# Giving a product a second pair of inputs instead of adding a trace, with four small edits around the router

## The reference

```
ctx    = ema(x, tau_ctx);  wg = sigmoid([x, ctx] @ Wg + bg);  gated = x * wg
mod    = 0.5 + sigmoid(gelu(x @ Wn1 + bn1) @ Wn2 + bn2)            # 8 values for each token
traces = ema(gated * mod[..., d], tau[d])  for d in 0..7
temporal = sum over d of traces[d] * softmax(blend)[d]
gate   = sigmoid(temporal @ Wtemp + btemp);  soma = gelu(x @ Wsoma + bsoma)
out    = (soma * gate) @ Wout;  z = layernorm(out) * gamma + beta
logits = z @ router.T;  top 8 of 64 experts, their softmax weights scaled to sum 1
expert e takes its first 128 tokens: silu(z @ Wgate) * (z @ Wup) @ Wdown, times the weight, added to each token
shared expert on all z;  x + routed + shared is the output
```

## Time and profile before

| what | us |
|---|---|
| median of three runs | 1110.4 |
| lowest and highest | 1106.49, 1114.75 |
| the profiled execution | 1111.76 |
| its span | 1110.0 |
| the conditioning pipeline in the trace | about 500 to 845 |
| the routed experts | about 852 to 1086 |

### The profile page before, as it was taken

The page is one execution under the profiler, slowest core; times in us unless marked ns, Lnnn a source line. Parts: engine busy times, 40 slices in busy tenths (PEclk is TensorE's granted clock), DMA queues, the critical chain, the costliest instruction groups (busy, mean ns, idle before and its releaser), DMA issues.

```text
span 1110.0 us, 14852 instructions
## 1 busy us (share of the span) xinstructions
PE 952.2 (86%) x4544; PEld 663.8 (60%) x4544; DVE 746.3 (67%) x1522; ACT 460.8 (42%) x835; POOL 667.0 (60%) x498
## 2 busy tenths in 40 slices
PE   5969899999999999987369889888688999889960
PEld 2534699899998999863125454444453665556640
DVE  2658466666666676524778999999876777667620
ACT  0320444555445544443446675757322222223320
POOL 1113444555445554315999999999852577777870
PEclk9989999999999999998689999999878999999995
DMA  4879234444344442134213742343259699996557
GB/s 153 276 261 349 63 77 113 90 89 95 87 118 86 89 100 39 21 66 105 96 38 96 245 150 69 114 138 117 90 167 320 179 262 264 259 254 144 94 72 156
DMA packets 93142, 155.46 MB, mean 140 GB/s; under 512 B 15784, under 2 KB 73328, under 8 KB 89936
## 3 DMA queue, kind: packets, MB, share of 16 engines
q1 hardware_dynamic: 51280, 90.61, 25.0%
q0 software_dynamic: 25296, 40.52, 20.3%
q10 hardware_dynamic: 16496, 23.49, 6.3%
HBM read 119.56 MB, written 43.42 MB: 147 GB/s over the span
## 4 chain that ended last, share of the span: by engine, by line
POOL 12%; issue 11%; PE 9%; DMA 7%; DVE 6%; ACT 2%; DVEq 2%; POOLq 2%; ACTq 0%
DMA odd_rows<-ys,slots 5%; POOL wide L652 4%; POOL wide L660 3%; DVE wide L1295 3%; PE bank L1685 3%; POOL xg L745 2%; DMA out<-ys,slots 2%; POOL out L752 1%; PE bank L1923 1%; DMA xg<-z_rows,slots 1%; POOL odd_rows L752 1%; POOLq L640 1%; ACT zrow L969 1%; ACT wide L919 1%; PE bank L1752 1%
## 5 line engine op out<-in xcount | busy, mean ns | idle before, releaser
L652 POOL TENSOR_TENSOR wide<-wide 128x1024 f32<-128x1024 f32 x64 | 156.6, 2461 | 31.8 <-issue 31.8
L1295 DVE TENSOR_TENSOR_SCAN wide<-bank,wide 128x512 f32<-128x512 f32 x128 | 149.4, 1210 | 22.3 <-POOL wide L652 22.1
L895 ACT ACTIVATE h_raw<-bank,b 128x512 f32<-128x512 f32 x128 | 88.1, 689 | 168.7 <-PE bank L1658 166.3
L1232 DVE TENSOR_TENSOR h_lo<-h_raw,h_hi 128x512 fp32r<-128x512 f32 x128 | 87.3, 692 | 91.8 <-ACT h_hi L899 91.8
L1673 PE MATMUL bank<-w_hi,h_hi 128*128 128x256 f32 x512 | 144.4, 282 | 0.1
L1673 PE MATMUL bank<-w_lo,h_hi 128*128 128x256 f32 x512 | 142.2, 278 | 0.0
L1673 PE MATMUL bank<-w_hi,h_lo 128*128 128x256 f32 x512 | 142.1, 278 | 0.0
L623 POOL DMA_INDIRECT x_rows<-ob,put x64 | 110.3, 1723 | 28.3 <-issue 16.0
L660 POOL TENSOR_TENSOR wide<-wide 128x1024 f32<-128x1024 f32 x46 | 108.4, 2358 | 11.9 <-issue 8.1
L919 ACT ACTIVATE wide<-wide,blend 128x512 f32<-128x512 f32 x128 | 84.0, 715 | 62.1 <-POOL wide L652 58.5
L1658 PE MATMUL bank<-ex_hi,w_hi 128*128 128x512 f32 x256 | 99.7, 389 | 2.5 <-issue 2.5
(11 more groups left out here) (242 smaller groups left out, 2002.6 us busy)
## 6 DMA issues: line engine op xcount, KB each, us to landing
wide<-in_mwp SPq DMA_DIRECT2D x40, 512.0 KB, 4.3
wide<-m_rows SPq DMA_DIRECT2D x16, 1024.0 KB, 4.8
w1s<-in_fW SPq DMA_DIRECT2D x8, 1024.0 KB, 5.0
w2s<-in_fW SPq DMA_DIRECT2D x8, 1024.0 KB, 5.3
own<-in_mwp SPq DMA_DIRECT2D x15, 512.0 KB, 4.9
head<-in_mwp SPq DMA_DIRECT2D x9, 512.0 KB, 4.3
xT<-in_xT ACTq DMA_DIRECT2D x8, 512.0 KB, 4.5
xt<-in_x ACTq DMA_DIRECT2D x8, 512.0 KB, 6.8
```

Source lines behind the costliest of these rows:

```text
L652: G.tensor_tensor(drive[n % DRIVES], gb[d % 2], md[d // HD][:, d % HD, :].unsqueeze(1).to_broadcast([P, CT, S]), ALU.mult).then_inc(c_u, 1)
L895: A.activation(h1_raw[f % 4][:, :], bank[:, 2 + f % 4, :], ACT.Gelu_apprx_tanh, bias=b1_0[:, bass.ds(e, 1), f]).then_inc(b_h, 1)
L1232: V.tensor_tensor(h1_lo[:, f, :], h1_raw[f % 4][:, :], h1_hi[:, f, :].bitcast(F32), ALU.subtract).then_inc(b_lo, 1)
L1295: o = V.tensor_tensor_scan(dst[:, c, :], decay[:, d:d + 1].to_broadcast([P, S]), drive[(D * b + d) % DRIVES][:, c, :], 0.0, ALU.mult, ALU.add)
```

## The change

Five edits come together.

1. Trace 7 is no longer added. `temp_in` takes `acc` and the ring buffer of trace 7 as four inputs of one accumulated product, the second pair with the same weights. Eight matmuls stand where four stood. Six adds stay for each sequence, one of them on VectorE. The buffer of trace 7 is given back by the product (`c_tem`) and not by an add. Two other waits, of SyncE's weight loads and of GpSimd's memsets in the last step, go from the last add to the last product.
2. Two small operations of `rstd_of` go from GpSimd to ScalarE (`moments`), ahead of `wg_out`.
3. The 0/1 mask of chosen experts is made on ScalarE with Sign and Relu (`chosen_out`) instead of a comparison and a copy on VectorE. For the last sequence VectorE writes it with one comparison.
4. The expert weights are stored without the division by their sum. The reciprocal of the sum goes into one more column, and each expert multiplies by it when it picks up its weight.
5. Rows of `z_rows` have 324 floats instead of 320.

```diff
-ZW = H + E1
+ZW = H + E1 + 4
...
 def added(b, d):
+    return level((D - 2) * b + d - 1)
...
     if b == B:
         weight_store(B - 2)
-        sp.wait_ge(c_add, added(B - 1, D - 1))
+        sp.wait_ge(c_tem, level(B - 1))
...
 def rstd_of(q):
-    pool.wait_ge(c_mv, level(q))
+    pool.wait_ge(c_mw, level(q))
     pool.wait_ge(c_no, level(q - 1, TT))
-    G.tensor_scalar(veps1[:, :], mv1[:, :, 1], 4 * EPS, None, ALU.add)
-    G.tensor_scalar(shift1[:, :], mv1[:, :, 0], -1.0, None, ALU.mult)
-    pool.drain()
...
     if on(b - 1) and b != B:
         add_trace(b - 1, 6)
-    if on(b - 1) and b != B:
-        add_trace(b - 1, 7)
...
+def moments(q):
+    act.wait_ge(c_mv, level(q))
+    act.wait_ge(c_no, level(q - 1, TT))
+    A.activation(veps1[:, :], mv1[:, :, 1], ACT.Copy, bias=4 * EPS)
+    A.activation(shift1[:, :], mv1[:, :, 0], ACT.Copy, scale=-1.0).then_inc(c_mw, 1)
...
+def chosen_out(q):
+    act.wait_ge(c_top, level(q))
+    A.activation(sign[:, :, :], rep[:, :, :], ACT.Sign, bias=far[:, :], scale=-1.0)
+    act.drain()
+    A.activation(chosen(q), sign[:, :, :], ACT.Relu).then_inc(c_ma, 1)
...
     if on(b):
         weighted(b, 7)
+    if on(b - 1):
+        moments(b - 1)
     if ahead(b + 1):
         wg_out(b + 1)
...
-    dve.drain()
-    V.tensor_tensor(mask[:, :, :], rep[:, :, :], lgp, ALU.not_equal).then_inc(c_top, 1)
-    dve.drain()
-    V.tensor_copy(mask_all[:, :, q * TT:(q + 1) * TT].rearrange("p e t -> p t e"), mask[:, :, :])
+    if q < B - 1:
+        o.then_inc(c_top, 1)
+    else:
+        dve.drain()
+        V.tensor_tensor(chosen(q), rep[:, :, :], lgp, ALU.not_equal).then_inc(c_top, 1)
...
-    V.tensor_tensor(mask[:, :, :], mask[:, :, :], ex[:, :, :], ALU.mult)
+    V.scalar_tensor_tensor(zrow[:, :, H:H + E1], rep[:, :, :], -1.0e38, ex[:, :, :], ALU.is_lt, ALU.mult)
...
-    V.reciprocal(wsum[:, :], wsum[:, :])
-    dve.drain()
-    V.tensor_tensor(zrow[:, :, H:ZW], mask[:, :, :], wsum[:, :].unsqueeze(2).to_broadcast([P, TT, E1]),
-                    ALU.mult).then_inc(c_zr, 1)
+    V.reciprocal(zrow[:, :, H + E1], wsum[:, :]).then_inc(c_zr, 1)
...
-    V.tensor_copy(share[i][:, :], xg1[e % ROWS][:, H + e:H + e + 1])
+    V.tensor_tensor(share[i][:, :], xg1[e % ROWS][:, H + e:H + e + 1], xg1[e % ROWS][:, H + E1:H + E1 + 1], ALU.mult)
...
 def temp_in(q):
-    pe.wait_ge(c_add, added(q, D - 1))
+    pe.wait_ge(c_add, added(q, D - 2))
+    pe.wait_ge(c_scan, level(D * q + D - 1))
     if q + 2 < B:
         pe.wait_ge(c_x1T, level(q + 2))
     pe.wait_ge(c_fin, level(q - 2))
-    project(4, wtemp, [acc[q % 2][:, 0, :], acc[q % 2][:, 1, :]]).then_inc(c_tem, 1)
+    last = trace[((D - 1) * q + D - 2) % TRACES]
+    project(4, wtemp, [acc[q % 2][:, 0, :], acc[q % 2][:, 1, :], last[:, 0, :], last[:, 1, :]]).then_inc(c_tem, 1)
```

More of the change, by code:

```diff
@@ L222, in build @@
         neg = sb("neg", [P, TT, E1])
-        mask = sb("mask", [P, TT, E1])
+        sign = sb("sign", [P, TT, E1])
+        far = sb("far", [P, 1])
         ex = sb("ex", [P, TT, E1])
@@ L282, in prep_start, with chosen @@
             return 4 * k - 8 - (0 if k < 4 else 1 if k == 4 else 2)
+        def chosen(q):
+            return mask_all[:, :, q * TT:(q + 1) * TT].rearrange("p e t -> p t e")
         def z_bank(q):
@@ L339, in build @@
         c_mdl = [sem(f"c_mdl{n}", 16) for n in range(2)]
+        c_mw = sem("c_mw")
+        c_ma = sem("c_ma")
         c_pad, e_pad = sem("c_pad", 0), sem("e_pad", 0)
@@ L710, in step @@
                 if b == B:
-                    pool.wait_ge(c_add, added(B - 1, D - 1))
+                    pool.wait_ge(c_tem, level(B - 1))
                     for r in range(FREED):
@@ L997, in step @@
                     exponentials(B - 2)
+                    chosen_out(B - 2)
                     shared_b_out(B - 2)
@@ L1000, in step @@
                     shared_out(B - 2)
+                    moments(B - 1)
                     normalise(B - 1)
@@ L1029, in step @@
                     exponentials(b - 2)
+                    chosen_out(b - 2)
                 if on(b):
@@ L1291, in scan_unit @@
                     n = (D - 1) * b + d - 1
-                    dve.wait_ge(c_add, level(n - TRACES))
+                    old, of = divmod(n - TRACES, D - 1)
+                    if of == D - 2:
+                        dve.wait_ge(c_tem, level(old))
+                    else:
+                        dve.wait_ge(c_add, added(old, of + 1))
                     dst = trace[n % TRACES]
@@ L1352, in pick @@
                     to_exponents()
+                dve.wait_ge(c_ma, level(min(q - 1, B - 2)))
                 for j in range(TT):
-                    V.match_replace(rep[:, j, :], top8[:, j, :], lgp[:, j, :], -3.0e38)
-                dve.drain()
-                V.tensor_tensor(mask[:, :, :], rep[:, :, :], lgp, ALU.not_equal).then_inc(c_top, 1)
-                dve.drain()
-                V.tensor_copy(mask_all[:, :, q * TT:(q + 1) * TT].rearrange("p e t -> p t e"), mask[:, :, :])
+                    o = V.match_replace(rep[:, j, :], top8[:, j, :], lgp[:, j, :], -3.0e38)
+                if q < B - 1:
+                    o.then_inc(c_top, 1)
+                else:
+                    dve.drain()
+                    V.tensor_tensor(chosen(q), rep[:, :, :], lgp, ALU.not_equal).then_inc(c_top, 1)
                 if q == B - 1:
@@ L1380, in route_weights @@
                 dve.wait_ge(c_zwt, level(q - 1, 16))
-                V.tensor_tensor(mask[:, :, :], mask[:, :, :], ex[:, :, :], ALU.mult)
+                V.scalar_tensor_tensor(zrow[:, :, H:H + E1], rep[:, :, :], -1.0e38, ex[:, :, :], ALU.is_lt, ALU.mult)
                 dve.drain()
-                V.tensor_reduce(wsum[:, :], mask[:, :, :], AX.X, ALU.add)
+                V.tensor_reduce(wsum[:, :], zrow[:, :, H:H + E1], AX.X, ALU.add)
                 dve.drain()
-                V.reciprocal(wsum[:, :], wsum[:, :])
-                dve.drain()
-                V.tensor_tensor(zrow[:, :, H:ZW], mask[:, :, :], wsum[:, :].unsqueeze(2).to_broadcast([P, TT, E1]),
-                                ALU.mult).then_inc(c_zr, 1)
+                V.reciprocal(zrow[:, :, H + E1], wsum[:, :]).then_inc(c_zr, 1)
             def finish(q):
@@ L1436, in drain_share @@
                 add_trace(B - 1, 6)
-                add_trace(B - 1, 7)
                 pick(B - 2)
@@ L1505, in front_only @@
             def front_only():
+                V.memset(zrow[:, :, H + E1 + 1:ZW], 0.0)
+                V.memset(far[:, :], -1.0e38)
                 ctx_scan(0, alpha)
@@ L1684, in project @@
                     for c in range(k):
-                        o = T.matmul(bank[:, o_banks + n, :], w[:, c, n * P:(n + 1) * P], src[c], start=(c == 0),
+                        o = T.matmul(bank[:, o_banks + n, :], w[:, c % w.shape[1], n * P:(n + 1) * P], src[c], start=(c == 0),
                                      stop=(c == k - 1))
```

## The result

The changed kernel takes 1117.45 us (median of 8 runs, 1114.55 to 1121.88). The kernel before, beside it on the same chip, takes 1110.34. The ratio is 1.0054, 95% interval 1.0033 to 1.0074: slower by half a per cent, 6.0 us by the ratio (the medians differ by 7.1). The forecast was 1117, and a change within 1%. The profiled execution took 1116.1 with a span of 1114.4.

What follows compares the result with a forecast made beforehand. GpSimd was taken to set the 37.17 us step, VectorE close behind; afterwards a ring of waits. Terms 0.6 + 3.8 - 0.9 - 0.2 + 3.4 - 0.9 + 0.3 = +6.1 gave 1118 profiled, 1117 predicted; 8-in-10 range 1108 to 1126.

Steps and rivals of the forecast that it cites:

- the forecast's ring: Layer 1 pipeline: waits from product through `gate_out`, drive 4, norm and `z_in` to the next product, 38.1 us against 37.2.
- product to drive 4: Full step: `gate_out` 7.14 us after the product's start, then 2.62 through `weighted(b,4)` to GpSimd's drive 4, 9.76 in all.
- the hold: Norm in a full step: VectorE's add 4 holds up GpSimd's drive 6 or the power, 0.95 us.
- four full steps, after less before: Second to sixth product: each full step about 0.95 us longer, +3.8 us in all.
- "gates late" rival: Full steps: VectorE's gates wait for `gate_out`, and each further VectorE wait lengthens every step; 1122 us, chance 0.06.
- The way back from the norm: From `z_in` to the next product: TensorE needs 11.95 us to be ready.
- The first interval: First to second product: product starts 2.25 us earlier, lasts 3.4 longer, with part low clock kept; +0.6 us.
- The clock rival: Products of sequences 0, 6 and 7 at half rate, each 3 us longer: 1123 to 1126 us, chance 0.11.
- The rival with GpSimd as the only bound: Six steps each lose 2.6 + 0.6 us and nothing takes GpSimd's place: 1095 us, chance 0.04.
- The bound by TensorE: Full step: TensorE's work of 33.27 + 3.41 = 36.68 us, so no step shorter than 36.7.
- The first rival: Full steps: relief is real and TensorE absorbs its work, steps 36.7 to 37.2, 1106 to 1112 us; chance 0.20.
- the rival's 2.2: Expert stretch: gathers cost more than their bytes, a tenth more DMA time each, 2.2 us, 1119 to 1120; chance 0.12.

Runs made afterwards that it cites:

- with `weighted(b, 4)` first: The changed kernel with ScalarE's `weighted(b, 4)` queued ahead of `gate_out(b - 1)`: 1108.66 us, ratio 0.9959 to the kernel before.
- with add 4 late: The changed kernel with VectorE's `add_trace(b, 4)` moved behind `scan_unit(b, 5)` and `gate_in(b + 1)`: 1111.48 us, ratio 1.0011 to the kernel before.
- The kernel with the product twice: The kernel before with all seven adds kept and the temporal product taking `acc` twice as inputs: 1134.03 us, ratio 1.0193.
- the kernel without the second pair: The kernel before with edits 2 to 5 alone, trace 7 still added on GpSimd: 1104.2 us, ratio 0.9914.
- The 1296 B rows: The kernel before with only `z_rows` lengthened from 320 to 324 floats: 1110.29 us, ratio 0.9994.
- 1536 B: The kernel before with only `z_rows` lengthened from 320 to 384 floats: 1111.58 us, ratio 1.0006.

## Why the prediction was right

Up to the normalisation the forecast's ring was the one that the profile shows, and most of its terms measured what I had summed.

| step of the prediction | foreseen | measured |
|---|---|---|
| product to drive 4 | 9.76 | 9.79 |
| drive 4 to the power, without the hold | 12.06 | 12.03 |
| the hold (power longer) | 0.95 | 0.96 |
| product to `z_in` | 26.17 | 26.18 |
| `z_in` to the next product | 11.95 | 12.20 |
| four full steps, after less before | +3.8 | +4.8 |
| first product, counted from the front's `soma_in` | -2.25 | -2.22 |
| first to second product | +2.85 | +1.25 |
| sixth to seventh | -0.9 | -0.7 |
| seventh to eighth | -0.2 | 0.0 |
| last product to first gather | +2.5 | +2.7 |
| first gather to the end | +0.3 | +0.5 |
| sum | +6.1 | +6.4 |

- *The full step* was mis-sized by 0.25. It is the "gates late" rival in small. VectorE's `gate_in` ended 0.21 after ScalarE was free for the `weighted` of the next sequence (its row at 734.48 above). `soma_out` behind them came late, and `shared_b_in` waited 1.33, where 0.94 is left with `weighted(b, 4)` first. I had given `gate_in` 0.7 us of slack ahead of TensorE's `soma_in`, which it kept (it ended at 734.44, `soma_in` started at 735.25), and had not asked when ScalarE needs it. The rows of the new mask sum to 1.83 on ScalarE (0.49 and 1.34), and the new multiply takes 1.77 on VectorE, but both lie beside other work.
- *The way back from the norm* had the right length and the wrong engine. I wrote that TensorE needs 11.95 from `z_in` to be ready. In the kernel before, a wait for `soma_out` lies inside that time:

```profile
738.44 1.95 PE L1762 MATMUL bank<-zT,ws_gu 128*128 128x512 f32 x4 [1.00 <-issue]
```

  The steady distance is the one from ScalarE's normalisation to `shared_b_in`. It is 8.39 before, with `weighted(b, 4)` first and with add 4 late, while `z_in` starts 6.40, 6.29 and 6.29 ahead of `shared_b_in`. After the change it is 8.72, with the 0.21 for `gate_in` in it. So ScalarE's queue (normalisation, four `weighted`, `z_out`, `soma_out`) carries the path there, and `z_in` has some 0.8 of slack, by my estimate from the rows (`soma_in` ended at 738.85, `soma_out` started at 739.68). No run moves `z_in` alone.
- *The first interval* was mis-sized by 1.6. I had the first product at 5.40 + 3.41 = 8.8, with the low clock of the earlier trace rows kept. TensorE's timeline after has it at 7.13, and the seventh at 7.09:

```profile
553.67 7.13 PE L1709 MATMUL bank<-wide,wtemp 128*128 128x512 f32 x16
...
782.96 7.09 PE L1709 MATMUL bank<-wide,wtemp 128*128 128x512 f32 x16
```

  The views by stretches over each, with the granted clock behind the five engines:

```profile
554.00:561.00 7.00, 7.00 (x17) 2.75 (x16) 3.68 (x4) 0.62 (x2) 6.21 (x3) 1.00 0.00 0
```

```profile
783.00:790.00 7.00, 7.00 (x19) 3.17 (x18) 5.40 (x17) 0.25 (x1) 6.63 (x3) 1.00 0.59 198
```

  The clock is 1.00, the level of 2.4 GHz, where the earlier trace rows had 0.50, 1.2 GHz. The idle time ahead of each product (2.25 and 2.48 in the earlier trace rows) went with the add. So I had applied to the seventh product the argument that I had not applied to the first. The kernel with the product twice keeps the idle time. Its first and seventh product:

```profile
557.70 8.83 PE L1685 MATMUL bank<-wide,wtemp 128*128 128x512 f32 x16 [2.46 <-POOL wide L660]
...
798.73 7.13 PE L1685 MATMUL bank<-wide,wtemp 128*128 128x512 f32 x16 [2.49 <-POOL wide L660]
```

  The first takes the 8.8 that I had counted, at a mean granted clock of 0.77 from 557.70 to 565.00. The seventh ran at 1.00 with 2.49 of idle time ahead of it. So the full clock that I took for the seventh came true, but the reason that I gave for it is not shown: there an idle time as long did not bring the low clock.
- *Luck.* The two errors, 1.0 more in the full steps and 1.6 less in the first interval, nearly cancel. My working gave 0.5 for the first interval, and the sum carries 0.6, which changes nothing. The ring of waits was right up to the normalisation; that the time came within 1 us of 1117 is in part chance. The clock rival fell. The rival with GpSimd as the only bound fell too: its 4.92 idle stands in front of drive 4.
- *The bound by TensorE.* I named 36.68 as its floor. Its busy time was 36.2 to 36.4, but with the wait for `soma_out` that it makes for itself the floor is 37.1: two different edits end there. My sum used busy time where a short ring of two engines was the limit: `wg_in` releases ScalarE's queue, and `shared_b_in` waits for its `soma_out`. It decided nothing, because the long ring is 38.4.
- *The first rival* (the relief is real and absorbed) held for the wrong edit. The relief of 1.15 a step is real in the kernel without the second pair, and it is the product's ring that hides it, not TensorE's work. Its range was also summed too low: with the +3.4 of the last product its terms give about -1 to +1, not -4 to +1.
- *The gathers.* The 1296 B rows had no measurable price; the interval still holds the 0.3 that I counted, and excludes the rival's 2.2. The 0.5 behind the first gather is within what this stretch differs by between profiles (255.1 to 263.0 over the fourteen kernels; 263.0 with rows of 1296 B, 258.1 with 1536 B).
- Between the two profiled executions the difference is only 4.3 us. Layer 1 began 1.97 earlier in the one after (its first `soma_in` at 542.52 against 544.49), and the change does not touch what lies before. It is within what executions differ by: over the fourteen traces, whose kernels are the same up to there, it begins anywhere from 540.14 to 545.04.

## What to carry to other kernels

An engine that is full loses its hold on the time once work leaves it, and then the longest ring of waits across engines sets the step, here product, `gate_out`, the work queued behind it, the norm, ScalarE's queue up to `soma_out`, product. Sum that ring before moving work, term by term, and look in each in-order queue for what stands behind the instruction that will now wait longer; here one exchange in ScalarE's order took back more than the half per cent that the whole change cost, though not all that the second pair cost. Cost the partial steps at the ends by themselves, since work that is hidden in a full step is on the path there, and time the parts of a joined change apart: four of five edits here gained 0.9%, and the fifth took back more than that.

## What the runs showed of the hardware

- *The shared port.* VectorE's add of two SBUF inputs takes what is left of GpSimd's drive when it comes, plus 1.1 us: 1.59 (0.51 left), 1.61, 3.08 (1.99 left), and 2.97 after the change, where it comes at 728.12 and the second drive ends at 730.00. There the power was asked for at 729.96, and it took 2.00 instead of 1.03: it ended 0.87 after the add. So a waiting add of VectorE gets the port ahead of GpSimd's next instruction. With `weighted(b, 4)` first the add came to a free port at 721.54 and took 1.23; the power, at 721.73, took 1.92 and ended 0.88 after it. The Trainium skill, SBUF — State Buffer, SBUF: two separate sides, says that whichever starts first gets the shared ports for the whole instruction; these rows agree, and that the waiting engine is next is from them alone.
- *A strided bf16 output on ScalarE.* Relu of 128x256 into `mask_all`, whose columns lie apart, took 1.34, and the Sign of as many elements into a contiguous f32 tile 0.49. A cast and a stride come together here, and no run tells them apart.
- *A DMA share of 0.97 to 0.99* over 110 us, in which 260 GB/s passed and then 269, and rows 20% longer without a measurable price (ratio 1.0006, at most 1.0024).
